# VectorE's masked copies as operations on two tensors, and a list schedule without a rule for a shared port

## The chip, the cores and the metric

The kernel runs on one core of a Trainium2 chip. The metric is the device time of one execution, in microseconds (us). The names of the engines are those of the profile: PE is TensorE (the matmuls, with PEld for its weight loads), DVE is VectorE, ACT is ScalarE, POOL is GpSimd, and SP is SyncE, which here issues the DMAs.

## The reference, cut to what matters

The input is 8 sequences of 512 tokens of width 256. Half a feed-forward block is added, then an attention block, then half of the same feed-forward block again. The "feed-forward block" holds an attention of its own, over the 16 heads of one token, whose keys and values are what the change touches.

```python
x = x + 0.5 * _L0_ffn_ref(_layernorm(x), ...)
x = x + _L0_attn_ref(_layernorm(x), ...)
x = x + 0.5 * _L0_ffn_ref(_layernorm(x), ...)

def _L0_ffn_ref(x, ...):                       # B=8 sequences, T=512, D=256, H=16, HD=16, E=8
    h = _rmsnorm(x, gamma1)
    q = (h @ Wq + bq).reshape(b, t, H, HD)
    kv = ((h @ Wdown + bdown) @ Wup + bup).reshape(b, t, H, 2 * HD)
    k, v = jnp.split(kv, 2, axis=-1)
    att = jax.nn.softmax(jnp.einsum('bthd,btgd->bthg', q, k) / sqrt(HD), axis=-1)
    out = jnp.einsum('bthg,btgd->bthd', att, v).reshape(b, t, D)
    x = x + (out @ Wo + bo)
    h2 = _rmsnorm(x, gamma2)
    gate = jax.nn.softmax(h2 @ Wg + bg, axis=-1)
    return x + jnp.einsum('btd,edf,bte->btf', h2, We, gate)
```

## The kernel before

**Jobs.** A job is one pass of the feed-forward block over one sequence. There are 16: jobs 0 to 7 before the attention block and 8 to 15 behind it. A job's 512 tokens are worked in two pairs of 128-token tiles, so that there are 32 pairs c = 0 to 31, with c = 2 * job + p. For each pair PE makes queries (step `q`, L448 with L453 for the bias) and keys and values (step `kv`, L448 with la and la_one). DVE turns them in blocks of 32x32: `q_turn` (L952) and `kv_turn` (L964 and L966, which write the tile kvcs).

**The masked copies.** The attention over heads is done with block-diagonal operands. The tile kvx holds, for each pair, eight blocks, and each block is a copy of half of kvcs, 128 partitions by 512 numbers, times a column of mask4, a 128x4 tile of zeros and ones. `EXPAND = "VPAAVPAV"` deals the eight copies out: three to DVE (step `expand_V`, L969), two to POOL (`expand_P`, L1390) and three to ACT (`expand_A`, L1165). When all eight are done PE multiplies queries and keys (`scores`, L613). DVE subtracts the maxima (`top`, L978 and L982), ACT exponentiates, PE turns (`turn_probs`, L708), ACT copies, PE multiplies by the values (`attend`, L624), and DVE divides (`mult`, L992 and L994). Output projection (`wo`), second norm and gating (`gate`, L448 with wg, `gateT` L755, `gate_sub` L1037 and L1039, `gate_soft` L1046 to L1055) follow.

**The experts.** The last product of a job has 16 `expert` steps, for four tiles i and four groups n, six matmuls of 512 columns each (L448, psum<-we,h). They use three PSUM banks in rotation: an expert step needs the bank that was filled three expert steps ahead of it to be read out. Steps with even n are read out by DVE (`add`, two instructions at L1067, which add into X), those with odd n by ACT (`y`, L1238). POOL then sums the y of a tile into X (`ysum`, L1421, L1423, L1426), and ACT's next `y` waits for that, since the tile y is reused.

**Other steps of POOL** that the prediction speaks of: `xs` (L1382, the first norm's scaling), `x1_base` (two at L1401, one at L1407), `norm` (L1344 to L1351, small operations and a power, L1349), `q_zero` (a memset, L1388), `we_lo` (L1372, eight operations that prepare the expert weights once). `half` is a DVE operation on two SBUF tensors (L1019). `h2_hi` (ACT, L1214) and `h2_lo` (DVE, L1027) copy the second norm's turned output out of PSUM, ahead of `gate` and the experts. In the attention block POOL's `normalise` (L1463) takes 3.9 us a time.

**What sets the order.** Each engine runs a fixed list of steps. The lists are made by a list scheduler on the host, `all_orders`, from a table of steps with an engine, a duration in ns and the steps that each waits for (`all_steps`). It goes forward in time and takes on each engine, of the steps that can start, the one with the longest chain behind it. The `expand_V` step stands in the table with 1900 ns. A rule named `port` lets no POOL step and none of the DVE steps `half`, `split_lo` and `expand_V` lie at the same time in the plan. The plan sets only the order: on the chip the semaphores decide when a step starts. The steps of the attention block follow one another by a list written out by formula; the feed-forward steps are placed around it.

## Time and profile before

| what | us |
|---|---|
| median of 3 runs | 1077.26 |
| lowest and highest | 1076.44, 1080.48 |
| the profiled execution, whole | 1075.92 |
| the profiled execution, span from its first instruction to its last | 1073.8 |

Busy time in the span: PE 1008.5 us (94%), DVE 864.4 (80%), POOL 746.5 (70%), ACT 648.4 (60%). A busy time is the union of an engine's instructions, so that an instruction that is held up while it runs counts as busy for all of it. TensorE's granted clock was 0.99 of full speed on average. A row of idle time names the instruction that waited and what released it last.

### The profile page before, as it was taken

To read this page: it belongs to the slowest core of one execution; us is meant where nothing else is said; L and a number is where in the kernel's file an instruction comes from. 1 tells how busy PE (TensorE), PEld (TensorE's weight loads), DVE (VectorE), ACT (ScalarE), POOL (GpSimd) and SP (SyncE) were. 2 spreads that over 40 slices of the span, in tenths; PEclk is the share of its full clock that TensorE was granted. 3 is DMA by queue.
4 is the path that set the end of the run, shared out by engine and by line. 5 is a ranking of instruction groups with operands and counts; after the bars stand their busy time and mean duration, and the time that the engine had idled before them with its cause. 6 is when DMAs were issued, how large, how long until landed. Compare 5 with 4: busy or idle time off the path is not lost.

```text
span 1073.8 us, 28494 instructions
## 1 busy us (share of the span) xinstructions
PE 1008.5 (94%) x11320; PEld 782.7 (73%) x11320; DVE 864.4 (80%) x1356; ACT 648.4 (60%) x1347; POOL 746.5 (70%) x743
## 2 busy tenths in 40 slices
PE   4789999999999989999999999877999999999997
PEld 3577888788788776666666666456878788788785
DVE  7888788787877459999999999988877787786852
ACT  4565564565654447777777777557654555655642
POOL 7667476675763449889889889995865574664544
PEclk9899999999999999999999999999999999999999
DMA  6110000000000000000000000000000000000000
GB/s 201 63 49 2 2 2 1 3 1 2 2 2 1 1 2 1 2 2 2 2 2 2 2 2 2 2 2 2 2 21 2 22 4 19 22 1 22 22 1 40
DMA packets 8410, 14.29 MB, mean 13 GB/s; under 512 B 2516, under 2 KB 6102, under 8 KB 8280
## 3 DMA queue, kind: packets, MB, share of 16 engines
q1 hardware_dynamic: 8280, 12.47, 3.5%
q8 instruction: 92, 1.51, 0.6%
q14 instruction: 38, 0.31, 0.1%
HBM read 8.28 MB, written 4.19 MB: 12 GB/s over the span
## 4 chain that ended last, share of the span: by engine, by line
PE 81%; DVE 8%; issue 5%; POOL 3%; ACT 1%; POOLq 0%; DVEq 0%; ACTq 0%
PE psum L448 54%; PE psum L816 5%; PE psum L826 5%; PE psum L842 4%; PE psum L613 3%; PE psum L624 3%; DVE late L1099 3%; DVE oT L1093 2%; PE psum L727 1%; PE psum L742 1%; PE psum L718 1%; PE psum L708 1%; PE psum L664 1%; DVE hT L1085 1%; POOL kvx L1463 1%
## 5 line engine op out<-in xcount | busy, mean ns | idle before, releaser
L448 PE MATMUL psum<-we,h 128*128 128x512 f32 x1536 | 396.6, 402 | 0.3 <-DVE X L1067 0.3
L448 PEld LDWEIGHTS psum<-we,h 128*128 128x128 f32 x1536 | 275.9, 188 | 59.4 <-issue 2.4
L1238 ACT ACTIVATE late<-psum,gate 128x256 f32<-128x256 f32 x256 | 107.2, 471 | 140.9 <-PE psum L448 96.2
L1421 POOL TENSOR_TENSOR late<-late 128x512 f32<-128x512 f32 x64 | 82.5, 1289 | 147.8 <-ACT late L1238 147.8
L1067 DVE SCALAR_TENSOR_TENSOR X<-psum,gate,X 128x256 f32<-128x256 f32 x256 | 122.8, 480 | 60.3 <-PE psum L448 48.3
L1288 ACT ACTIVATE kvx<-psum 128x1024 f32<-128x1024 f32 x128 | 131.3, 1026 | 64.3 <-PE psum L826 64.1
L1093 DVE TENSOR_REDUCE oT<-psum 128x128 fp32r<-128x1024 f32 x128 | 154.6, 1220 | 16.5 <-PE psum L816 16.1
L1099 DVE TENSOR_REDUCE late<-kvx 128x256 f32<-128x2048 f32 x64 | 145.7, 2277 | 0.0
L1463 POOL TENSOR_TENSOR kvx<-kvx,late 128x2048 f32<-128x2048 f32 x32 | 125.7, 3928 | 20.7 <-ACT late L1295 20.7
L1463 POOL TENSOR_TENSOR late<-kvx,late 128x2048 f32<-128x2048 f32 x32 | 125.2, 3914 | 15.8 <-ACT late L1295 15.8
L826 PE MATMUL psum<-oT,neg_id 128*128 128x512 f32 x256 | 89.1, 429 | 15.2 <-DVE oT L1093 14.6
L1165 ACT ACTIVATE kvx<-kvcs,mask 128x512 f32<-128x512 f32 x96 | 63.5, 741 | 6.8 <-PE psum L624 3.4
L826 PEld LDWEIGHTS psum<-oT,neg_id 128*128 128x128 f32 x256 | 40.5, 188 | 31.4 <-DVE oT L1093 22.3
L969 DVE TENSOR_SCALAR kvx<-kvcs,mask 128x512 f32<-128x512 f32 x96 | 63.0, 710 | 0.2
L1390 POOL TENSOR_SCALAR kvx<-kvcs,mask 128x512 f32<-128x512 f32 x64 | 47.1, 750 | 17.9 <-PE psum L624 10.7
L1180 ACT ACTIVATE at<-psum 64x256 f32<-64x256 f32 x128 | 48.5, 379 | 14.6 <-PE psum L708 13.3
L816 PEld LDWEIGHTS psum<-late 32*128 32x128 f32 x1024 | 37.1, 187 | 27.3 <-issue 27.3
L816 PEld LDWEIGHTS psum<-kvcs 32*128 32x128 f32 x1024 | 36.7, 185 | 26.6 <-issue 23.9
L1426 POOL TENSOR_TENSOR X<-X,late 128x256 f32<-128x256 f32 x64 | 47.2, 737 | 9.5 <-DVE X L1067 0.4
L448 PEld LDWEIGHTS psum<-wq,hT 128*128 128x128 f32 x384 | 50.7, 192 | 2.5
L816 PE MATMUL psum<-kvcs 32*128 32x128 f32 x1024 | 49.3, 295 | 3.1 <-ACT kvx L1288 2.2
L448 PE MATMUL psum<-wq,hT 128*128 128x256 f32 x384 | 51.2, 283 | 0.0
(153 smaller groups left out, 2010.3 us busy)
## 6 DMA issues: line engine op xcount, KB each, us to landing
X<-in_L_attn_hidden_states SPq DMA_DIRECT2D x8, 512.0 KB, 5.8
out<-X SPq DMA_DIRECT2D x8, 512.0 KB, 2.7
X<-in_L_ffn_We SPq DMA_DIRECT2D x2, 1024.0 KB, 10.6
kvx<-in_L_ffn_Wq SPq DMA_DIRECT2D x1, 256.0 KB, 3.0
kvx<-in_L_ffn_Wup SPq DMA_DIRECT2D x2, 128.0 KB, 3.1
kvx<-in_L_ffn_Wo SPq DMA_DIRECT2D x1, 256.0 KB, 4.2
X<-in_L_attn_Wk SPq DMA_DIRECT2D x1, 256.0 KB, 2.9
X<-in_L_attn_Wq SPq DMA_DIRECT2D x1, 256.0 KB, 3.2
```

Source lines behind the costliest of these rows:

```text
L448: ins = e.matmul(out_ap, l, r, start=(n == 0 and not opened), stop=(n == len(terms) - 1), skip_group_check=opened)
L816: ins = e.matmul(psum[:, pair(half) + bank, n * HQN:(n + 1) * HQN], qk[b % 2][rows, 1, hg, m * P:(m + 1) * P], qk[b % 2][rows, 0, hg, q0:q ...
L826: ins = e.matmul(psum[:, bank, :].rearrange("p (g n) -> p g n", n=HQN), neg_id[:, :], mr[g // 2 % 2][:, queries(g)].unsqueeze(1).to_broadc ...
L969: expand(e, k, "V", lambda o, src, m_: e.tensor_scalar(o, src, m_, None, ALU.mult))
L1067: e.scalar_tensor_tensor(out=xi, in0=psum[:, u % 3, w * D:(w + 1) * D], scalar=gate[k % 2][:, i, 2 * n + w:2 * n + w + 1], in1=xi, op0=ALU ...
L1093: e.tensor_reduce(mr[g // 2 % 2][:, queries(g)], heads(g), AX.X, ALU.max).then_inc(a_max, 1)
L1099: e.tensor_reduce(rec[u % 2][:, :], a_ex[u % EXR][:, :, :], AX.X, ALU.add).then_inc(a_total, 1)
L1165: expand(e, k, "A", lambda o, src, m_: e.activation(o, src, ACT.Copy, scale=m_))
L1238: e.activation(y[:, n // 2 * 2 + w, :], psum[:, u % 3, w * D:(w + 1) * D], ACT.Copy, scale=gate[k % 2][:, i, 2 * n + w:2 * n + w + 1]).the ...
L1288: e.activation(a_ex[u % EXR][:, queries(g), :], heads(g), ACT.Exp, scale=float(D) ** -0.5).then_inc(a_exp, 1)
L1421: own.step(e.tensor_tensor(y[:, 0:2, :], y[:, 0:2, :], y[:, 2:4, :], ALU.add))
L1463: e.tensor_tensor(prob[u % 2][:, :, :].rearrange("p g n -> p n g"), a_ex[u % EXR][:, :, :], rec[u % 2][:, :].unsqueeze(2).to_broadcast([P, ...
```

## The change

Two things change. DVE's three masked copies for each pair become `tensor_tensor` multiplications: the first operand is the half of kvcs as before, the second is the mask column, repeated 512 times by a stride of zero, in place of a per-partition scalar. Destination, count and size stay. And the rule `port` is taken out of the list scheduler, so that it may place DVE's `half`, `split_lo` and `expand_V` beside any POOL step. The duration table is as it was, 1900 ns for `expand_V` too. Six lines fewer stand above, so line numbers behind are lower by 6: L969 is L963, L1390 is L1384.

```diff
-    free = dict.fromkeys((*engines, "port"), 0)
+    free = dict.fromkeys(engines, 0)
...
-    def port(p):
-
-        return steps[p][0] == "POOL" or p[0] in ("half", "split_lo", "expand_V")
-
     def possible(p):
-        start = max(ready[steps[p][0]][p], free[steps[p][0]], free["port"] if port(p) else 0)
+        start = max(ready[steps[p][0]][p], free[steps[p][0]])
...
-        if port(p):
-            free["port"] = end[p]
...
                 elif name == "expand_V":
-                    expand(e, k, "V", lambda o, src, m_: e.tensor_scalar(o, src, m_, None, ALU.mult))
+                    expand(e, k, "V", lambda o, src, m_: e.tensor_tensor(o, src, m_.unsqueeze(2).to_broadcast([P, NR, HD]), ALU.mult))
```

The lists of DVE, PE, ACT and POOL all change. The first place is DVE in the middle jobs, from the turning of a job's first keys and values on. Before (L1067 is `add`, L969 the copies, L1027 `h2_lo`, L978 and L982 `top`):

```order
L964 STREAM_TRANSPOSE kvcs<-psum 128x16x32
L966 STREAM_TRANSPOSE kvcs<-psum 128x16x32
L952 STREAM_TRANSPOSE qc<-psum 128x16x32
L1067 SCALAR_TENSOR_TENSOR X<-psum,gate,X 128x256 x4
L964 STREAM_TRANSPOSE kvcs<-psum 128x16x32
L966 STREAM_TRANSPOSE kvcs<-psum 128x16x32
L952 STREAM_TRANSPOSE qc<-psum 128x16x32
L969 TENSOR_SCALAR kvx<-kvcs,mask 128x32x16 x3
L1027 SCALAR_TENSOR_TENSOR h<-psum,gam,h 128x256 x4
L969 TENSOR_SCALAR kvx<-kvcs,mask 128x32x16 x3
L978 TENSOR_REDUCE mx<-psum 128x32
L982 TENSOR_TENSOR late<-psum,mx 128x512
```

And DVE at the same place in the changed kernel (L1061 is `add`, L963 the copies, L1021 `h2_lo`, L972 and L976 `top`):

```order
L946 STREAM_TRANSPOSE qc<-psum 128x16x32
L1061 SCALAR_TENSOR_TENSOR X<-psum,gate,X 128x256 x2
L963 TENSOR_TENSOR kvx<-kvcs,mask 128x32x16 x3
L958 STREAM_TRANSPOSE kvcs<-psum 128x16x32
L960 STREAM_TRANSPOSE kvcs<-psum 128x16x32
L946 STREAM_TRANSPOSE qc<-psum 128x16x32
L1061 SCALAR_TENSOR_TENSOR X<-psum,gate,X 128x256 x2
L1021 SCALAR_TENSOR_TENSOR h<-psum,gam,h 128x256 x4
L972 TENSOR_REDUCE mx<-psum 128x32
L976 TENSOR_TENSOR late<-psum,mx 128x512
L963 TENSOR_TENSOR kvx<-kvcs,mask 128x32x16 x3
L1061 SCALAR_TENSOR_TENSOR X<-psum,gate,X 128x256 x2
```

The first pair's copies have moved up, ahead of the second `kv_turn`, and the second pair's have moved behind the first pair's `top`. Between the first `kv_turn` and the third `add` the set of steps is the same.

The second place is PE in the same stretch, from the turning of the second norm's output (L742, L736) on. L613 and L607 are `scores`, L708 and L702 `turn_probs`. Before:

```order
L742 MATMUL psum<-ident,late 128x128 x8
L448 MATMUL psum<-we,h 128x512 x12
L613 MATMUL psum<-kvx,qc 32x64 x32
L448 MATMUL psum<-we,h 128x512 x6
L448 MATMUL psum<-h,wg 8x512 x6
L613 MATMUL psum<-kvx,qc 32x64 x32
L755 MATMUL psum<-ident,ct 128x8 x4
L664 MATMUL psum<-ident,xs 128x128 x4
L448 MATMUL psum<-we,h 128x512 x6
```

PE there in the changed kernel:

```order
L736 MATMUL psum<-ident,late 128x128 x8
L442 MATMUL psum<-we,h 128x512 x6
L607 MATMUL psum<-kvx,qc 32x64 x32
L442 MATMUL psum<-we,h 128x512 x6
L442 MATMUL psum<-h,wg 8x512 x6
L442 MATMUL psum<-we,h 128x512 x6
L702 MATMUL psum<-ident,late 128x128 x4
L749 MATMUL psum<-ident,ct 128x8 x4
L658 MATMUL psum<-ident,xs 128x128 x4
L442 MATMUL psum<-we,h 128x512 x6
```

Ahead of the last expert step shown, the second `scores` is gone (it comes right behind it), and a `turn_probs` has come in.

The third place is POOL in the opening, around the copies of the third pair (L1390, L1384). Before:

```order
L1407 TENSOR_TENSOR late<-late,b_out 128x512
L1372 TENSOR_TENSOR we<-X,we 128x512
L1388 MEMSET qc 64x32x16
L1372 TENSOR_TENSOR we<-X,we 128x512 x3
L1390 TENSOR_SCALAR kvx<-kvcs,mask 128x32x16 x2
L1388 MEMSET qc 64x32x16
L1318 TENSOR_TENSOR wg<-raw_g,wg 128x16
L1372 TENSOR_TENSOR we<-X,we 128x512 x4
L1390 TENSOR_SCALAR kvx<-kvcs,mask 128x32x16 x2
```

POOL there in the changed kernel:

```order
L1366 TENSOR_TENSOR we<-X,we 128x512
L1444 TENSOR_SCALAR la_one<-la 64x512
L1366 TENSOR_TENSOR we<-X,we 128x512 x2
L1382 MEMSET qc 64x32x16
L1366 TENSOR_TENSOR we<-X,we 128x512 x3
L1384 TENSOR_SCALAR kvx<-kvcs,mask 128x32x16 x2
L1382 MEMSET qc 64x32x16
L1366 TENSOR_TENSOR we<-X,we 128x512 x2
L1384 TENSOR_SCALAR kvx<-kvcs,mask 128x32x16 x2
```

Six of the eight `we_lo` operations now stand ahead of the third pair's copies, where four did.

## Rows read from the trace of the kernel before

**Rows 1.** Busy times of the page, and a stretch (PE, PEld, DVE, ACT, POOL)

```profile
PE 1008.5 (94%) x11320; PEld 782.7 (73%) x11320; DVE 864.4 (80%) x1356; ACT 648.4 (60%) x1347; POOL 746.5 (70%) x743
...
176.00:219.00 43.00, 43.00 (x468) 35.23 (x468) 35.02 (x75) 24.52 (x60) 28.22 (x41) 1.00 0.01 2
```

**Rows 2.** Durations of two lines of DVE (ns: min/median/max)

```profile
L969 DVE TENSOR_SCALAR kvx<-kvcs,mask x96: 466/486/6749, 27.0 to 1011.3; 128x512 f32<-128x512 f32 x96
...
L886 DVE TENSOR_TENSOR wq<-kvx,wq x1: 693/693/693, 7.6 to 7.6; 128x512 fp32r<-128x512 f32 x1
```

**Rows 3.** Timeline of the opening: start, length, instruction, [idle before, releaser]

```profile
40.34 7.54 DVE L969 TENSOR_SCALAR kvx<-kvcs,mask 128x512 f32<-128x512 f32 x3
...
41.89 4.92 POOL L1372 TENSOR_TENSOR we<-X,we 128x512 fp32r<-128x512 f32 x4
...
48.10 1.93 PE L613 MATMUL psum<-kvx,qc 128*32 128x64 f32 x64 [5.97 <-issue]
```

**Rows 4.** Timeline: DVE operations on two SBUF tensors, and POOL beside them

```profile
63.55 1.29 POOL L1318 TENSOR_TENSOR aw<-X,aw 128x512 fp32r<-128x512 f32 x1 [1.73 <-ACT aw L1107]
...
64.51 0.87 DVE L1019 SCALAR_TENSOR_TENSOR X<-late,X 128x512 f32<-128x512 f32 x1
...
82.74 1.66 POOL L1349 TENSOR_TENSOR rs<-rs,half_neg 128x8 f32<-128x8 f32 x1
84.47 0.54 POOL L1351 TENSOR_TENSOR negm<-rs,negm 128x8 f32<-128x8 f32 x1
...
83.74 1.21 DVE L1019 SCALAR_TENSOR_TENSOR X<-late,X 128x1024 f32<-128x1024 f32 x1
```

**Rows 5.** Timeline at 314 us, where DVE's and POOL's copies coincide

```profile
314.32 2.41 DVE L969 TENSOR_SCALAR kvx<-kvcs,mask 128x512 f32<-128x512 f32 x3
314.70 1.75 POOL L1390 TENSOR_SCALAR kvx<-kvcs,mask 128x512 f32<-128x512 f32 x2
```

**Rows 6.** Timeline of DVE in a middle job

```profile
177.29 1.14 DVE L964 STREAM_TRANSPOSE kvcs<-psum 128x512 f32<-128x512 f32 x1
...
180.16 0.93 DVE L1067 SCALAR_TENSOR_TENSOR X<-psum,gate,X 128x256 f32<-128x256 f32 x2
181.69 1.00 DVE L1067 SCALAR_TENSOR_TENSOR X<-psum,gate,X 128x256 f32<-128x256 f32 x2 [0.60 <-PE psum L448]
...
185.59 1.98 DVE L969 TENSOR_SCALAR kvx<-kvcs,mask 128x512 f32<-128x512 f32 x3
...
189.11 1.36 DVE L969 TENSOR_SCALAR kvx<-kvcs,mask 128x512 f32<-128x512 f32 x3
...
191.78 0.99 DVE L1067 SCALAR_TENSOR_TENSOR X<-psum,gate,X 128x256 f32<-128x256 f32 x2
```

**Rows 7.** Timeline of PE in the same job, around the expert step that waits for that `add`

```profile
193.18 1.10 PE L613 MATMUL psum<-kvx,qc 128*32 128x64 f32 x64
194.21 0.41 PE L755 MATMUL psum<-ident,ct 8*128 8x8 f32 x4
...
194.97 1.63 PE L448 MATMUL psum<-we,h 128*128 128x512 f32 x6
196.44 0.60 PE L708 MATMUL psum<-ident,late 128*128 128x128 f32 x4
196.79 1.63 PE L448 MATMUL psum<-we,h 128*128 128x512 f32 x6
```

**Rows 8.** Timeline of POOL and ACT in the same job

```profile
181.50 1.43 POOL L1390 TENSOR_SCALAR kvx<-kvcs,mask 128x512 f32<-128x512 f32 x2
...
185.93 0.84 ACT L1238 ACTIVATE late<-psum,gate 128x256 f32<-128x256 f32 x2 [2.39 <-POOL X L1426]
```

**Rows 9.** Timeline of the return to the jobs

```profile
737.38 1.44 DVE L969 TENSOR_SCALAR kvx<-kvcs,mask 128x512 f32<-128x512 f32 x3
...
745.11 1.27 DVE L969 TENSOR_SCALAR kvx<-kvcs,mask 128x512 f32<-128x512 f32 x3
...
746.59 1.10 PE L613 MATMUL psum<-kvx,qc 128*32 128x64 f32 x64 [0.71 <-issue]
```

## The prediction

> **What bounds the kernel now.** I read the busy times and a table of stretches first. PE is busy 1008.5 us of 1073.8. In a middle job of 43 us it has no idle time at all, while DVE works 35.0 us of it and POOL 28.2 [rows 1]. So there a slower DVE costs nothing until one certain PE step has to wait for it, and then each microsecond of that wait is a microsecond of the whole. There are eight such equal periods, from 133 to 305 us and from 821 to 993 us, each with the copies of two pairs.
>
> The line of the copies comes next: 96 instructions, median 486 ns, longest 6749 ns [rows 2]. The long one is in the opening. DVE's three copies there take 7.54 us, POOL's chain of `we_lo` runs to 46.81 us, and PE stands for 5.97 us until the `scores` behind those copies can start at 48.10 [rows 3]. So the copies of today are held up by POOL. The question is whether the new ones are too, and what the new order makes of it.
>
> **The single operation.** The one two-tensor operation of 128x512 from SBUF in the trace takes 0.69 us, against 0.486 [rows 2]. Three copies took 1.27 us where nothing disturbed them [rows 9], which is 3 x 0.486 less 0.19 of overlap. Three new ones then take 3 x 0.69 - 0.19 = 1.88 us, 0.6 us more for each pair. All 32 pairs give 19.5 us more of DVE's work; only what lies on PE's path counts.
>
> **Is the new operation held up by POOL?** The trace has two DVE operations on two SBUF tensors beside POOL. At 64.51 us a `half` of 128x512 took 0.87, where the undisturbed two-tensor operation of that size took 0.69 [rows 2]: it ended at 65.38, and POOL's operation had ended at 63.55 + 1.29 = 64.84, 0.54 us ahead. In the other direction POOL's L1351, a 128x8 operation of 0.20 us, took 0.54 and ended at 85.01, when DVE's `half` had ended at 84.95 [rows 4]. So either makes the other wait, and DVE's 128x512 operation holds what they share for some 0.55 us. The shorter copy of today holds it less: at 314 us three copies and two of POOL's took turns for 2.41 us, POOL's two from start to end 1.75 [rows 5]. With 486 - 690/2 = some 0.28 us held for each DVE copy there, one of POOL's holds (1.75 - 2 x 0.28)/2 = 0.60 us.
>
> The Trainium skill (SBUF — State Buffer, "Who interferes with whom") says the same of these kinds: a VectorE instruction with two SBUF inputs contends with a GpSimd instruction that reads SBUF, and one that only writes it leaves it alone. It also says that the holder keeps the port for its whole instruction. The trace does not bear that out for every kind: `half` began at 83.74 inside POOL's L1349 (82.74 to 84.40) and took 1.21 us for 128x1024, less than twice 0.69 [rows 4]. By the page it would have waited the 0.66 us until POOL's end. None of the terms below rests on POOL's L1349.
>
> **The middle jobs, the largest term.** Follow the `add` that ends at 192.77 [rows 6]. The third expert step behind its own, which starts at 194.97 [rows 7], needs its bank. Between the first `kv_turn` at 177.29 and this `add` the new order has the same DVE steps. So their time is 192.77 - 177.29 = 15.48, less the copies' 1.98 and 1.36 and 0.60 of idle time: 11.54 us of other work [rows 6]. In PE's new order a `scores` is gone ahead of the expert step (194.21 - 193.18 = 1.03) and a `turn_probs` has come in (196.79 - 196.44 = 0.35) [rows 7]. PE gets there at 194.97 - 1.03 + 0.35 = 194.29. Both sets of copies together may take 194.29 - 177.29 - 11.54 = 5.46 us before PE stands.
>
> Undisturbed they take 3.76, and PE never waits. But they are not undisturbed. The first set moves up to 181.0, right behind the `add` of 180.16, and POOL's copies of the same pair start at 181.50 [rows 6, 8]. They take turns: 0.5 until POOL's running operation ends, 3 x 0.55 for DVE's and 2 x 0.60 for POOL's between them, 3.35 us. The second set meets `x1_base` or POOL's second copies, which stand there back to back in the new order: the same 3.35. The sum of 6.70 is 1.24 us over. On POOL's side each wait of 0.55 moves what is behind: `ysum` comes 1.65 us later, the `y` of ACT that waited for it (185.93, idle 2.39) as well [rows 8], and with it `h2_hi` and `h2_lo`, which stand behind that `y` and ahead of the second copies. DVE reaches `h2_lo` only 0.75 later by itself, so this adds up to 0.9. PE loses 1.24 to 2.1 us a period. I take 1.6, nearer to the end that DVE's own rows give. Eight periods: **+12.8 us**. The ends are 0 (nothing held, then 3.76 under 5.46) and 8 x 2.1 = 17.
>
> **The opening.** `we_lo` is POOL's chain of 1.23 us operations (4.92 / 4) [rows 3], and in the new order six of the eight stand ahead of the third pair's POOL copies. DVE's third set arrives inside that chain again. If they take turns, it lasts about 3 x (1.23 + 0.55) = 5.3 us in place of 7.54, but it begins later, since the first two pairs' sets are longer by 0.6 to 2 us each on a DVE that works nearly without a break there, and POOL's copies come two `we_lo` (2.5 us) later. The fourth set adds 0.6. I take **0**, with -5 (no stall) and +4 (a stall as long as today's, begun later) as ends.
>
> **The return from attention.** PE waits 0.71 us for the fourth set at 745.11; 1.27 becomes 1.88: +0.6. The third, at 737.38, took 1.44 [rows 9] beside POOL's copies; with one turn of POOL's it is 1.88 + 0.5, +0.9. **+1.5 us**, ends -1 (the new order has the first `scores` there in an idle stretch) and +3. The attention block has no copies, and its own steps keep their order: 0.
>
> **Sum.** 12.8 + 0 + 1.5 = +14.3 us on a span of 1073.8. Around the span lie 1075.9 - 1073.8 = 2.1 us, and the median is 1.3 above the profiled execution: 1077.3 + 14.3 = **1091.6 us**.
>
> **The rivals.** Taking turns, as summed, has 0.48: 1081 to 1100.
>
> No hold: a mask column that is read over and over might be fetched once, and then nothing is shared. For it speaks that no row has such an operand with both inputs in SBUF. The middle jobs then cost 0 and the long stall goes, which is up to the 5.97 us of PE, less 0.6 for each of the four sets of the opening, and the return costs 1.2. 1077.3 - 6 + 2.4 + 1.2 = 1074.9, same. 0.15. If the new order's earlier copies also bring PE's other waits of opening and return in, some 5 us more go: 1070, faster. 0.10.
>
> Half held: the two sets meet POOL's only once each in a period. Then they take 2 x 2.5 = 5.0 us, under 5.46, and only the chain over `ysum` is left, 0.6 us a period: 1077.3 + 5 + 1.5 = 1084. 0.15. It decides at 5.46 us for both sets.
>
> Starved: in the opening POOL had eight operations in a row while a copy waited (6749 ns). If that happens in the middle jobs, behind POOL's copies and `ysum`, each period costs 1.5 us more and the opening 4: 1091.6 + 12 + 4 = 1108. Against it: at 314 us they took turns [rows 5]. 0.12.
>
> **How the numbers follow.** A difference of 0.5% (5.4 us) is about what a measurement of this kernel can tell from none. Faster by more, under 1071.9: 0.11. Within: 0.17, from no hold and the lower edge of half held. Slower: 0.72. The range from 1073 to 1101 takes in no hold, half held and turns with their ends, and leaves the 0.10 and most of the 0.12 out.
>
> **What would show it.** DVE's copies last 3.0 to 3.5 us a set in the middle jobs and not 1.9; no single one is under 0.68. PE has 1 to 2 us of idle time in each middle period, released by `add` (L1061) or `h2_lo` (L1021), and the period is 44 to 45 us. If PE's middle periods stay at 43.0, the step on the hold or the 5.46 us is wrong. If PE waits, but for ACT's `y` or for `scores`, the place is wrong and the size a coincidence.

## The result

The changed kernel is slower, by more than the forecast said and beyond its range. It was timed twice, each time beside the kernel before on the same chip.

| | after, median (lowest to highest) | before, median | ratio, 95% interval |
|---|---|---|---|
| first | 1104.57 (1101.68 to 1106.85, 4 runs) | 1078.87 | 1.0232, 1.0184 to 1.0279 |
| again (`e5_after_again`) | 1103.15 (1102.00 to 1105.02, 4 runs) | 1081.97 | 1.0204, 1.0176 to 1.0232 |

That is 21 to 26 us where 14 were forecast. The profiled execution of the changed kernel took 1102.69 us with a span of 1100.6, against 1073.8 before.

The busy times of its page, and the stretch of one middle period, from the first expert step of job 4 to that of job 5 (columns as in [rows 1]):

```profile
PE 1018.2 (93%) x11320; PEld 786.9 (71%) x11320; DVE 893.0 (81%) x1356; ACT 649.3 (59%) x1347; POOL 777.9 (71%) x743
...
245.66:289.90 44.24, 43.37 (x467) 35.14 (x466) 37.56 (x75) 24.61 (x60) 30.42 (x41) 1.00 0.01 2
```

Against [rows 1], DVE is busy 28.6 us more and POOL 31.4 us more, though POOL has not one instruction more: it is held up. The period is 44.24 us, and PE has 0.87 us of visible idle time in it.

Where the time went, by the starts of the first expert step of the jobs (us). Before and after were each profiled twice, the second time as `e12_before_again` and `e5_after_again`, for which I had written:

> The kernel after once more, unchanged, on the chip of the runs beside it: 1102 to 1108 if the op and the order together cost what they did, where each alone cost 0.4 and 3.0 us; its first expert step at 68 to 73 us and its middle period at 44.2 us. A first expert step far from 71.5 would say that part of the +6.2 of the opening belongs to the one execution that was profiled.

> The kernel before once more, unchanged, for a second trace of it, since its runs lie between 1075 and 1085 us and the profiled one took 1075.9. If the opening and the attention are what differs from run to run: the middle period is 42.9 us again, and the first expert step lies at 65 to 69 us. If an execution differs anywhere else, the period shows it.

| stretch | before | after | more |
|---|---|---|---|
| to the first expert step of job 0 | 65.3, 64.9 | 71.5, 71.6 | +6.4 |
| jobs 0 to 2 | 82.0, 82.0 | 84.6, 84.7 | +2.7 |
| jobs 2 to 6 | 173.0, 173.2 | 178.2, 178.9 | +5.4 |
| jobs 6 to 7 | 33.6, 33.7 | 35.3, 35.3 | +1.7 |
| jobs 7 to 8, with the attention block | 399.1, 406.0 | 402.1, 400.3 | not told apart |
| jobs 8 to 10 | 82.6, 82.6 | 86.1, 86.1 | +3.5 |
| jobs 10 to 14 | 173.3, 173.6 | 178.3, 178.6 | +5.0 |
| jobs 14 to 15 | 34.7, 34.7 | 34.3, 34.3 | -0.4 |

The sum is 24 us. The +5.4 and +5.0 are not spread evenly: of four periods two lose 1.3 us each, one (jobs 2 to 3, or 12 to 13) loses 2.4 to 3.1, and the last loses 0.1 or nothing (44.4 us for jobs 5 to 6, against 44.3). Every stretch but one repeats to within 0.7 us. The exception is the one with the attention block, which differs by 7 us between two executions of the same kernel; in the slower of the two the granted clock was 0.67 from 710 to 730 us, where it had been 1.00. That fits the times of before, which lie anywhere from 1075 to 1086 us, though two traces do not show it for all of them. So I compare stretches, not totals, where a few microseconds matter.

The copies and the lines beside them, in after (ns: min/median/max):

```profile
L963 DVE TENSOR_TENSOR kvx<-kvcs,mask x96: 676/684/6929, 24.4 to 1032.3; 128x512 f32<-128x512 f32 x96
```
```profile
L1384 POOL TENSOR_SCALAR kvx<-kvcs,mask x64: 713/729/1745, 28.2 to 1035.8; 128x512 f32<-128x512 f32 x64
```
```profile
L1044 DVE TENSOR_SCALAR gs<-gs x18: 168/440/1807, 74.0 to 1073.5; 128x4 f32<-128x4 f32 x14, 128x2 f32<-128x2 f32 x4
```

A single copy costs what the forecast took, 0.68 to 0.69 us. POOL's copies are held to 1.75 us. And a third line stands out that the forecast never named: L1044, a DVE operation on 128x4 numbers in `gate_soft` (L1050 before), which takes up to 1.8 us.

### The profile page after: what moved, and what is told of

Same layout as the page of the kernel before. It is cut to its first block, busy times and chain, and to the rows that moved or that the text cites. A ratio compares the mean times of both kernels' runs of the same rounds, so it can differ in the third digit from the quotient of the medians.

```text
span 1100.6 us, 28494 instructions
## 1 busy us (share of the span) xinstructions
PE 1018.2 (93%) x11320; PEld 786.9 (71%) x11320; DVE 893.0 (81%) x1356; ACT 649.3 (59%) x1347; POOL 777.9 (71%) x743
## 4 chain that ended last, share of the span: by engine, by line
PE 55%; DVE 18%; POOL 13%; issue 9%; ACT 4%; POOLq 0%; DVEq 0%; ACTq 0%
PE psum L442 33%; PE psum L810 5%; PE psum L820 4%; PE psum L836 4%; DVE oT L1087 2%; DVE late L1093 2%; POOL xs L1376 2%; PE psum L618 2%; POOL rs L1343 2%; DVE kvx L963 2%; POOL kvx L1384 1%; PE psum L721 1%; DVE h L1021 1%; PE psum L607 1%; POOL late L1415 1%
## 5 line engine op out<-in xcount | busy, mean ns | idle before, releaser
L1415 POOL TENSOR_TENSOR late<-late 128x512 f32<-128x512 f32 x64 | 82.6, 1290 | 152.1 <-ACT late L1232 152.1
L1061 DVE SCALAR_TENSOR_TENSOR X<-psum,gate,X 128x256 f32<-128x256 f32 x256 | 121.8, 477 | 51.3 <-PE psum L442 40.0
L963 DVE TENSOR_TENSOR kvx<-kvcs,mask 128x512 f32<-128x512 f32 x96 | 79.8, 884 | 0.6
L1384 POOL TENSOR_SCALAR kvx<-kvcs,mask 128x512 f32<-128x512 f32 x64 | 64.5, 1022 | 15.8 <-PE psum L618 11.5
L820 PEld LDWEIGHTS psum<-oT,neg_id 128*128 128x128 f32 x256 | 40.5, 188 | 31.4 <-DVE oT L1087 22.3
L442 PEld LDWEIGHTS psum<-wq,hT 128*128 128x128 f32 x384 | 53.2, 201 | 2.6
L607 PE MATMUL psum<-kvx,qc 128*32 128x64 f32 x2048 | 37.8, 229 | 18.3 <-DVE kvx L963 7.6
L607 PEld LDWEIGHTS psum<-kvx,qc 128*32 128x32 f32 x2048 | 33.2, 116 | 30.0 <-issue 28.2
```

What stands on the lines that cost most here:

```text
L442: ins = e.matmul(out_ap, l, r, start=(n == 0 and not opened), stop=(n == len(terms) - 1), skip_group_check=opened)
L607: ins = e.matmul(psum[32 * j:32 * j + 32, keys[0], (2 * a4 + odd) * HALF:(2 * a4 + odd + 1) * HALF], queries_[:, r, :, :], keys[1][:, r, 0 ...
L820: ins = e.matmul(psum[:, bank, :].rearrange("p (g n) -> p g n", n=HQN), neg_id[:, :], mr[g // 2 % 2][:, queries(g)].unsqueeze(1).to_broadc ...
L963: expand(e, k, "V", lambda o, src, m_: e.tensor_tensor(o, src, m_.unsqueeze(2).to_broadcast([P, NR, HD]), ALU.mult))
L1061: e.scalar_tensor_tensor(out=xi, in0=psum[:, u % 3, w * D:(w + 1) * D], scalar=gate[k % 2][:, i, 2 * n + w:2 * n + w + 1], in1=xi, op0=ALU ...
L1415: own.step(e.tensor_tensor(y[:, 0:2, :], y[:, 0:2, :], y[:, 2:4, :], ALU.add))
```

## Experiment 1: each half of the change alone

The first question was which half does it. `e1_op_only` has the new operation and the rule, so that every engine keeps the order of before:

```diff
-                    expand(e, k, "V", lambda o, src, m_: e.tensor_scalar(o, src, m_, None, ALU.mult))
+                    expand(e, k, "V", lambda o, src, m_: e.tensor_tensor(o, src, m_.unsqueeze(2).to_broadcast([P, NR, HD]), ALU.mult))
```

> The kernel before with the operation changed alone: VectorE's copies are tensor_tensor with the mask repeated, and the port rule stays in the list schedule, so every engine has the order of before. If the moved order did the harm (my theory now: the surplus comes from POOL and VectorE steps that now stand side by side), this is within 4 us of before (1079 +- 4), a set of three copies lasts about 1.9 to 2.1 us alone and no VectorE copy takes over 2 us but the one of the opening. If the operation itself is dear (rival), it shows most of the +26: about 1095 to 1105.

`e2_rule_only` has the order of after and the old operation (the same line the other way round).

> The kernel after with the old operation: tensor_scalar copies in the order without the port rule. By the theory that the order does the harm, whatever the operation: 1095 to 1110, with the long first copy of the opening (6 to 8 us) and TENSOR_SCALAR L1044 (128x4) at 1 us on average as in after. By the rival that the new operation does it (it lets no POOL operation in between): within 5 us of before, 1074 to 1084.

Measured beside before at 1081.53 (19 runs): `e1_op_only` 1081.91 us (10 runs), ratio 1.0013 (0.9991 to 1.0036); `e2_rule_only` 1084.55 us (10 runs), ratio 1.0033 (1.0015 to 1.0051). So neither half costs the 21 us: 0.4 and 3.0 for each alone. My theory that the order does the harm whatever the operation fell here, and so did its rival. The stretches show it more closely (us more than the mean of the two traces of before):

| stretch | new operation alone | new order alone | both |
|---|---|---|---|
| to the first expert step | +4.1 | +3.8 | +6.4 |
| jobs 0 to 2 | 0 | +1.4 | +2.7 |
| jobs 2 to 6 and 10 to 14 | -2.2 | +0.4 | +10.5 |
| jobs 6 to 7 | +1.4 | +1.7 | +1.7 |
| jobs 8 to 10 | 0 | +2.4 | +3.5 |
| jobs 14 to 15 | +0.7 | -0.4 | -0.4 |

The new order alone costs 9 us here and 3 in the medians. The difference lies in the stretch with the attention block: it was 398.8 us in `e2_rule_only`, as short as the shorter one of before, and the ten times of that kernel lie within 2.4 us. The new operation alone costs 4.0 us here and 0.4 in the medians; its stretch with the attention block was 403.4 us, inside the 7 us of before, and cannot settle that. Outside the middle the two halves about add up: 15.0 us in sum against 13.8 for both, and to within 1.5 us in each stretch. In the middle they don't: alone they give -2.2 and +0.4, together +10.5. A middle period is 42.91 us in before, 42.65 with the operation alone, 42.63 with the order alone, and 44.24 with both:

```profile
236.47:279.12 42.65, 42.65 (x473) 35.15 (x467) 35.75 (x75) 24.46 (x60) 29.45 (x41) 1.00 0.01 2
```
```profile
238.70:281.33 42.63, 42.63 (x468) 35.12 (x466) 35.69 (x75) 24.48 (x60) 28.75 (x41) 1.00 0.01 2
```

(first `e1_op_only`, then `e2_rule_only`.) Both are bound by PE: 42.6 us of it, with no idle time. Each half's own delays on DVE and POOL are covered there. (Before has no visible idle time in its period either, and is 0.26 us longer: one expert step, at 241.74, starts 0.22 us later than in `e1_op_only`, where it is 244.87, by the same reckoning as in the next section. What it waits for there I have not traced.)

## How a middle period loses 1.6 us

`e2_rule_only` and after have the same instructions in the same order on every engine and differ in one operation. So their rows can be laid side by side, each counted from the start of its period (238.70 and 245.66). DVE and POOL around the two sets of copies of the period, and PE. First `e2_rule_only`:

```profile
227.41 1.35 POOL L1376 TENSOR_SCALAR xs<-X,rs,negm 128x256 f32<-128x256 f32 x2 [0.18 <-POOL negm L1345]
228.01 1.90 DVE L963 TENSOR_SCALAR kvx<-kvcs,mask 128x512 f32<-128x512 f32 x3
...
238.04 1.75 DVE L963 TENSOR_SCALAR kvx<-kvcs,mask 128x512 f32<-128x512 f32 x3
239.10 1.50 POOL L1395 TENSOR_SCALAR late<-X,rs,negm 128x256 f32<-128x256 f32 x2
239.72 0.99 DVE L1061 SCALAR_TENSOR_TENSOR X<-psum,gate,X 128x256 f32<-128x256 f32 x2
...
241.37 1.64 PE L442 MATMUL psum<-we,h 128*128 128x512 f32 x6
242.38 1.28 POOL L1415 TENSOR_TENSOR late<-late 128x512 f32<-128x512 f32 x1
242.94 1.10 PE L607 MATMUL psum<-kvx,qc 128*32 128x64 f32 x64
243.05 0.63 DVE L1044 TENSOR_SCALAR gs<-gs 128x4 f32<-128x4 f32 x1
...
247.82 0.60 PE L702 MATMUL psum<-ident,late 128*128 128x128 f32 x4
```

And after:

```profile
233.91 2.15 POOL L1376 TENSOR_SCALAR xs<-X,rs,negm 128x256 f32<-128x256 f32 x2 [0.18 <-POOL negm L1345]
234.51 2.09 DVE L963 TENSOR_TENSOR kvx<-kvcs,mask 128x512 f32<-128x512 f32 x3
...
245.44 2.32 DVE L963 TENSOR_TENSOR kvx<-kvcs,mask 128x512 f32<-128x512 f32 x3
245.50 1.74 POOL L1384 TENSOR_SCALAR kvx<-kvcs,mask 128x512 f32<-128x512 f32 x1
247.22 1.50 POOL L1395 TENSOR_SCALAR late<-X,rs,negm 128x256 f32<-128x256 f32 x2
247.68 0.99 DVE L1061 SCALAR_TENSOR_TENSOR X<-psum,gate,X 128x256 f32<-128x256 f32 x2
...
248.82 1.64 PE L442 MATMUL psum<-we,h 128*128 128x512 f32 x6 [0.25 <-DVE X L1061]
250.02 1.81 DVE L1044 TENSOR_SCALAR gs<-gs 128x4 f32<-128x4 f32 x1
250.51 1.29 POOL L1415 TENSOR_TENSOR late<-late 128x512 f32<-128x512 f32 x1
250.65 1.10 PE L607 MATMUL psum<-kvx,qc 128*32 128x64 f32 x64 [0.18 <-issue]
...
255.90 0.63 PE L702 MATMUL psum<-ident,late 128*128 128x128 f32 x4 [0.23 <-ACT late L1163]
```

The copies do not take turns one for one. DVE's second set is 2.32 us long, not 3.35: the first two copies run back to back (682 and 684 ns) while one POOL copy waits through both (1.74 us for 0.72). POOL gets in once, ahead of the third, which takes 1119 ns. PE's expert step that waits for L1061 starts at 248.82 - 245.66 = 3.16 us instead of 241.37 - 238.70 = 2.67: 0.49 lost. The next `scores` starts at 4.99 instead of 4.24: another 0.26.

L1415, the first addition of the job's last `ysum`, starts at 4.85 instead of 3.68. L1044 starts at 250.02, while POOL's L1401 still runs to 250.09. A memset of POOL and L1415 follow without a pause, and L1044 stands through them: it is done at 251.83, when L1415 has ended (251.80). The gate is ready late, and so are `add` and `y`; PE's `turn_probs` starts 0.38 later still. In before the same small operation took 0.17 to 0.25 us in all 18 places.

The first set of the period holds POOL too: `xs` L1376 x2 took 2.15 us beside it, against 1.35 in `e2_rule_only`. What follows from that is a chain over three engines, first in `e2_rule_only`, then in after:

```profile
277.43 1.10 PE L607 MATMUL psum<-kvx,qc 128*32 128x64 f32 x64
277.71 1.66 DVE L1021 SCALAR_TENSOR_TENSOR h<-psum,gam,h 128x256 fp32r<-128x256 f32 x4 [1.43 <-ACT h L1208]
...
279.95 1.54 PE L442 MATMUL psum<-h,wg 128*8 128x512 f32 x6
```
```profile
285.11 0.84 ACT L1232 ACTIVATE late<-psum,gate 128x256 f32<-128x256 f32 x2 [3.83 <-POOL X L1420]
...
285.64 1.10 PE L607 MATMUL psum<-kvx,qc 128*32 128x64 f32 x64
285.84 1.57 ACT L1208 ACTIVATE h<-psum,gam 128x256 fp32r<-128x256 f32 x4
...
286.71 1.66 DVE L1021 SCALAR_TENSOR_TENSOR h<-psum,gam,h 128x256 fp32r<-128x256 f32 x4 [2.11 <-ACT h L1208]
...
288.52 1.55 PE L442 MATMUL psum<-h,wg 128*8 128x512 f32 x6 [0.17 <-DVE h L1021]
```

POOL's `ysum` ends late, ACT's `y` waits for it, `h2_hi` stands behind that `y`, `h2_lo` waits for `h2_hi`, and `gate` on PE waits for `h2_lo`: 0.10 at the `scores` ahead of it, and 0.36 at `gate`. The five places give 0.49 + 0.26 + 0.38 + 0.10 + 0.36 = 1.59 us, the whole difference of 44.24 and 42.63. (In the last period of each four the difference is 0.2 us: the same delays arise, and PE makes them up again near the end of it.)

PE's idle time in brackets adds up to much less. A wait of a few tenths between matmuls lies largely inside PE's busy time, which grew by 0.74 us for the same matmuls. Two traces of one order are needed to find it.

## Experiment 2: the places one by one

**L1044.** `e3_no_halving` is after without this operation:

```diff
-                    own.step(e.tensor_scalar(gs[:, 0, own_t], gs[:, 2, own_t], 0.5, None, ALU.mult))
...
-                    e.tensor_tensor(g[:, own_t, :], gl[:, own_t, :], gs[:, 0, own_t].unsqueeze(2).to_broadcast([P, n, E]),
-                                    ALU.mult).then_inc(s_gate, 1)
+                    e.scalar_tensor_tensor(out=g[:, own_t, :], in0=gl[:, own_t, :], scalar=0.5,
+                                           in1=gs[:, 2, own_t].unsqueeze(2).to_broadcast([P, n, E]),
+                                           op0=ALU.mult, op1=ALU.mult).then_inc(s_gate, 1)
```

> The kernel after, with the small TENSOR_SCALAR L1044 of gate_soft (gs x 0.5, 128x4; 18 of them took 16 us in after where they took 3.4 us before) folded into the multiplication behind it, now a scalar_tensor_tensor with the scalar 0.5. Same result. If that operation's wait for a POOL operation beside it sets when the gate is ready, and so a middle period of 44.2 us (before 42.9), this gives back 0.8 to 1.2 us in each of 14 periods: 1090 to 1094. If the period is set by POOL's chain over ysum (L1420, y L1232, h2_hi, h2_lo), nothing is given back: 1102 to 1107. If the wait only moves to the next VectorE operation L1049: 1100 to 1106 and L1049 of 1.5 us.

1099.1 us against 1081.53 (ratio 1.0163, 1.0125 to 1.0201), middle period 43.87. The delay at `turn_probs` is gone (0.38), the other four are there as before. So the wait of L1044 has its price, but less than the 0.8 to 1.2 that I expected, and it is one place of five.

**POOL's place for `x1_base`.** `e8_ysum_first` moves one step on POOL alone:

```diff
+        line = orders["POOL"]
+        for s in range(2, 2 * B):
+            base, last = ("x1_base", s, 1), ("ysum", s - 2, NT - 1)
+            if s not in (B, B + 1) and line.index(base) < line.index(last):
+                line.remove(base)
+                line.insert(line.index(last) + 1, base)
```

> The kernel after with one step moved on POOL alone: x1_base(s, 1) (L1395 x2, L1401, 2.8 us) stands behind the last ysum of job s-2 instead of ahead of it, as in before; the other engines keep after's order. If the harm of the new order is that this step, with the copies that hold it up, stands ahead of the ysum that y L1232 and with it h2_hi and the next expert step wait for: a middle period of 42.7 to 43.3 us and a kernel of 1083 to 1092. If the place of that step is innocent: 44.0 to 44.3 and 1101 to 1107.

1098.43 us against 1081.97 (1.0157, 1.0131 to 1.0183), middle period 43.6. Gone are the delay at `turn_probs` (0.38) and the one at `scores` (0.26); 0.49, 0.10 and 0.36 stay. So the place of `x1_base` explains 0.6 us of the 1.6, not most of it as I expected. It explains the same 0.38 as L1044 does, since L1044 stood through a `ysum` that `x1_base` had made late.

**POOL's load.** `e7_pool_half` leaves out half of each of POOL's copies from set 4 on:

```diff
+                    if who == "P" and c >= 4:
+                        rows = slice(rows.start, rows.start + NR // 4)
```

> The kernel after with POOL's copies (L1384) of half the rows from set 4 on; the other half is left out, so the output of the later jobs is not the reference's. VectorE's copies are untouched. POOL gains 0.35 us a copy, 1.4 us a period. If the middle period is set by POOL's lateness (copies held through two or three of VectorE's, x1_base, ysum L1420, y L1232, h2_hi): it falls from 44.2 to 42.7 to 43.1, and the kernel to 1084 to 1090. If it is set by VectorE's own chain (the second set of 2.3 us ahead of add L1061): it stays at 43.9 to 44.3, and the kernel at 1100 to 1105.

1094.77 us against 1081.97 (1.0124, 1.0098 to 1.0151), middle period 43.4. The delays at `gate` and at the `scores` ahead of it are gone (0.46 together), and the first two are less than half (0.21 and 0.11 for 0.49 and 0.26). So the chain over `ysum` and `h2_lo` is real and costs 0.46, and it was the part that the forecast had described. The expected 42.7 to 43.1 was too low, since 0.37 at `turn_probs` stayed.

**DVE's second set ahead of `add`.** `e10_add_first` is e8 with one step more moved, on DVE:

```diff
+        line = orders["DVE"]
+        for s in range(2, 2 * B):
+            copies, add = ("expand_V", 2 * s + 1), ("add", s - 2, NT - 1, 2)
+            if s not in (B, B + 1) and line.index(copies) < line.index(add):
+                line.remove(add)
+                line.insert(line.index(copies), add)
```

> e8_ysum_first (middle period 43.6 us, 1098.4 us) with one more step moved, on VectorE: the last add of a job (L1061) stands ahead of the second set of copies instead of behind it. In after, and still in e8, the expert step that waits for this add starts 0.47 us later than in the kernel with the old operation, because the set ahead of the add takes 2.3 us where it took 1.75. If that is so: a middle period of 43.1 to 43.3 us and 1090 to 1096 for the kernel. If the set is not what the add waits for: 43.5 to 43.7 and 1097 to 1100.

1101.04 us against 1079.26 (1.0209, 1.0172 to 1.0246), middle period 43.5. The 0.49 at the expert step is gone, as expected. But the set comes 1 us later and meets `ysum` instead of `x1_base`. DVE and POOL in `e10_add_first`:

```profile
245.78 3.51 DVE L975 TENSOR_TENSOR kvx<-kvcs,mask 128x512 f32<-128x512 f32 x3
246.09 1.51 POOL L1427 TENSOR_TENSOR late<-late 128x512 f32<-128x512 f32 x1
...
247.68 1.07 POOL L1429 TENSOR_TENSOR late<-late 128x256 f32<-128x256 f32 x1
```

Now they do take turns for its last two copies, the set lasts 3.51 us, and `scores` is 0.33 late instead. The loss moved, and some other periods became longer (46.6 us for jobs 12 to 13, 45.5 in after). The place was right and the remedy worthless.

## Experiment 3: who gets in, and when

In after two of DVE's copies went through in a row while a POOL copy stood; beside `ysum` they took turns. `ysum` is where POOL waits for its own result between two operations. So `e9_gap` gives DVE such a wait:

```diff
+                    if who == "V" and ins is not None:
+                        dve_own.step(ins)
+                        e.wait_ge(dve_own.sem, dve_own.n)
```

> The kernel after with a wait of VectorE for its own copy ahead of the second and third copy of each set (L963), so that a copy is finished before the next is issued. If POOL's copies (L1384, 1.74 us in the second set of a middle job, 0.72 alone) are held because VectorE issues its copies back to back and takes the port again each time: with the waits they get in after one copy, at most 1.3 us each, and a set lasts 3 to 3.4 us, copy and copy in turns, so that the middle period is no shorter than 44.2. If the hold has nothing to do with the issue: L1384 keeps 1.7 us and the sets last 2.5 us (0.1 us more for each wait).

One run: 1105.04 us, middle period 44.0 to 44.1. In the middle jobs the longest POOL copy falls from 1.74 to 1.21 us, but more of them are held, 24 of 32 where 16 were:

```profile
L1388 POOL TENSOR_SCALAR kvx<-kvcs,mask x64: 712/1148/1303, 27.7 to 1035.9; 128x512 f32<-128x512 f32 x64
```

The sets last 2.70 and 2.77 us, less than the 3 us I expected for turns, but copies of 0.86 and 1.09 us show that POOL gets in between. So an engine that waits for its own result lets the other in; the sum of the two is about the same.

The reverse, that an engine which issues back to back keeps the other one out, is not shown, and often does not hold. In `e1_op_only` the same two POOL copies and three DVE copies meet, and none waits for a result:

```profile
234.69 1.97 POOL L1390 TENSOR_SCALAR kvx<-kvcs,mask 128x512 f32<-128x512 f32 x2
235.40 2.40 DVE L969 TENSOR_TENSOR kvx<-kvcs,mask 128x512 f32<-128x512 f32 x3
```

There the second POOL copy stood through one DVE copy only (1.28 us), and got in ahead of the second. In the other direction I took, in the trace of after, every place where a POOL operation ended beside a DVE copy that was being held, and the next POOL operation followed without a pause. There are 32. At 25 of them the copy got in, and six of the other seven belong to the one copy of 6.93 us in the opening. Where POOL paused for 0.08 to 0.23 us, the copy got in every time, in all the traces.

The long copy is in the opening. `e6_we_wait` is the kernel before with a wait of POOL between its `we_lo`:

```diff
                     e.wait_ge(s_hi, 7 + kk)
+                    if we_done:
+                        e.wait_ge(s_we, we_done)
+                    we_done += 1
```

> The kernel before with one thing added: ahead of each we_lo (POOL L1372, 128x512) POOL waits on the semaphore that the we_lo before it raises, so that it has finished before the next one is issued. In before, a VectorE copy of the opening took 6.7 us while eight POOL operations ran without a wait between them. If a waiting VectorE operation gets in only where POOL itself waits for something: that copy takes 1.3 to 2.6 us, the expert steps start 3 to 6 us earlier, and the kernel takes 1075 to 1079 where before takes 1081. If POOL's own gaps make no difference (rival): the copy still takes 5 to 8 us, and the kernel takes 1081 to 1083.

```profile
39.93 2.62 DVE L969 TENSOR_SCALAR kvx<-kvcs,mask 128x512 f32<-128x512 f32 x3
...
42.19 5.77 POOL L1376 TENSOR_TENSOR we<-X,we 128x512 fp32r<-128x512 f32 x4
42.75 1.10 PE L613 MATMUL psum<-kvx,qc 128*32 128x64 f32 x64 [1.03 <-DVE kvx L969]
```

The set of 7.54 us in [rows 3] takes 2.62, and PE's `scores` starts at 42.75 instead of 48.10. But the set is nearly over when the first of these `we_lo` starts (39.93 + 2.62 = 42.55, against 42.19). Its first two copies got in at 40.55 and 41.87 us, after a POOL copy and after a memset, and no new wait stands there. The set also began 0.4 us earlier than in before, against POOL's copies. So this run does not show that a held operation gets in only where the other engine waits; `e14_after_we_wait` below shows more. The worth of it is another thing. 1078.51 us against 1081.97 has a ratio of 0.9992 (0.9957 to 1.0027), so I ran it again:

> e6 once more (before with the wait between the we_lo): its first expert step came 2.0 us earlier than in before, but its ten times lay between 1072 and 1087. If that is all it gives: 2 us below before, ratio 0.997 to 0.999, and perhaps not to be told from no change. If the later opening has a price at the aw splits, which now stand beside PE's wait: 1.000.

1080.28 us against 1078.37, ratio 1.0020 (0.9997 to 1.0043), first expert step at 65.8. Of the 5.3 us that `scores` gained, 2.0 reached the first expert step in one execution and none in the other. Up to there PE is idle for 22.2 and 23.3 us, against 25.6 in before, but busy for 41.1 and 42.5 against 39.7 for the same 626 matmuls: 10.2 and 10.6 us of PE's work fell into stretches with the granted clock at half, where 7.0 did in before. It is no faster kernel. Nor is the same wait with the new operation in the order of before:

> The order of before, the new operation, and the wait between the we_lo of e6: meant as the fastest of those built so far. The new operation costs nothing in the middle there (42.7 us a period against 42.9), and the wait took the long copy of the opening from 6.7 to 1.4 us and the time to 1078.5 against 1082.0. If both hold together: 1076 to 1080 with before at 1082, ratio 0.994 to 0.998. If the gain of e6 was chance: 1081 to 1083.

1083.19 us against 1079.26, ratio 1.0042 (1.0014 to 1.0069), slightly above both ranges that I gave. No version that I ran beats the kernel before.

## Experiment 4: the opening

In after the first expert step comes 6.4 us late. `e4_rule_opening` keeps the rule for steps that the plan starts ahead of 60 us:

```diff
+        if port(p) and start < 60000:
+            start = max(start, free["port"])
```

> The kernel after with the port rule kept for steps that the list schedule starts before 60 us of its own time: the opening has the order of before on every engine up to about 75 us of the plan, the rest nearly the order of after. New copies throughout. If the opening's +6.2 us (first expert step 71.5 against 65.3) and the +2.6 of jobs 0 to 2 come from the moved order there: the first expert step is back at 65 to 66 and the kernel takes 1093 to 1099. If they come from the new operation: no change, 1101 to 1107.

1101.91 us against 1081.53 (1.0188, 1.0150 to 1.0225), first expert step at 68.8. So only 2.7 us came back, and the rest is the operation's: the first expert step is at 69.2 in `e1_op_only` and at 68.9 in `e2_rule_only`. Here the two halves come near to adding up (4.1 and 3.8 for 6.4). Not all of it is waiting. Up to the first expert step PE is idle for 25.6 us in before and for 29.6 in after; it is busy for 39.7 and 41.9. Some 1.1 us of that is work that moved: 64 matmuls more, as many as one `scores` has, stand ahead of this step in the new order. The rest goes with TensorE's granted clock: 8.7 us of PE's work fell into stretches with the clock at half in after, 7.0 in before. With the operation alone the clock is the larger part: `e1_op_only` has before's 626 matmuls up to there, and PE is idle for 26.1 us but busy for 43.0, of which 12.4 fell into such stretches. The trace of after shows two places of the waiting, POOL's steps ahead of its first copies and the third set:

```profile
24.29 2.55 POOL L1395 TENSOR_SCALAR late<-X,rs,negm 128x256 f32<-128x256 f32 x2
24.44 2.14 DVE L963 TENSOR_TENSOR kvx<-kvcs,mask 128x512 f32<-128x512 f32 x3
...
26.99 1.26 POOL L1401 TENSOR_TENSOR late<-late,b_out 128x512 f32<-128x512 f32 x1
...
30.30 1.94 PE L607 MATMUL psum<-kvx,qc 128*32 128x64 f32 x64 [4.73 <-POOL kvx L870]
...
42.63 3.75 POOL L1366 TENSOR_TENSOR we<-X,we 128x512 fp32r<-128x512 f32 x3
44.30 8.13 DVE L963 TENSOR_TENSOR kvx<-kvcs,mask 128x512 f32<-128x512 f32 x3
46.37 1.41 POOL L1384 TENSOR_SCALAR kvx<-kvcs,mask 128x512 f32<-128x512 f32 x2
...
48.20 2.48 POOL L1366 TENSOR_TENSOR we<-X,we 128x512 fp32r<-128x512 f32 x2
```

`e13_base_later` puts `x1_base(0, 1)` back behind POOL's first copies, and `e14_after_we_wait` is after with the wait of e6:

```diff
+        orders["POOL"].remove(("x1_base", 0, 1))
+        orders["POOL"].insert(orders["POOL"].index(("expand_P", 1)) + 1, ("x1_base", 0, 1))
```

> The kernel after with one step moved on POOL: x1_base(0, 1) (L1395 x2, L1401; 24.3 to 28.3 us in after, where one L1395 took 2.0 us beside VectorE's copies) stands behind POOL's first two sets of copies, as in before, instead of ahead of them. PE idles 4.7 us in after until POOL's first copies are done (scores(0) at 30.3 us). If this step is what holds them: scores(0) at 26 to 27.5 us, and the first expert step 1.5 to 3.5 us earlier than in after, 68 to 70. If another thing is late next (the copies of set 2, held through eight POOL operations): scores(0) as early, but the first expert step at 71 to 72.

> The kernel after with POOL's wait between the we_lo, as in e6. The first copy of set 2 took 6.9 us in after behind eight POOL operations. If the wait lets it in, as it did in e6: that copy at 1 to 2.7 us and the first expert step at 68 to 70, as much earlier as in before with the same wait (2 to 3 us). If it does not: 71 to 72.

First expert steps at 68.7 and 69.3 us, against 71.5, one run each: both as expected. In e13 PE's first `scores` starts at 28.11 instead of 30.30, earlier but not by as much as expected. In e14 the third set lasts 4.04 us instead of 8.13, with single copies of 1.77 and 1.75:

```profile
45.30 4.04 DVE L963 TENSOR_TENSOR kvx<-kvcs,mask 128x512 f32<-128x512 f32 x3
46.66 1.53 POOL L1370 TENSOR_TENSOR we<-X,we 128x512 fp32r<-128x512 f32 x1
48.17 2.37 POOL L1388 TENSOR_SCALAR kvx<-kvcs,mask 128x512 f32<-128x512 f32 x2
```

The first of these copies got in at the first pause of POOL, between the `we_lo` that ended at 46.52 and the one at 46.66; the first copy of the set of 8.13 us stood through seven POOL operations without one. The second got in at 48.19 with no pause at all (46.66 + 1.53, and POOL's next starts at 48.17). In e13 a set in the opening takes turns one for one, copies of 0.83, 1.78 and 1.75 us, beside POOL operations that follow one another without a pause:

```profile
31.43 4.21 DVE L965 TENSOR_TENSOR kvx<-kvcs,mask 128x512 f32<-128x512 f32 x3
31.87 1.54 POOL L1403 TENSOR_TENSOR late<-late,b_out 128x512 f32<-128x512 f32 x1
33.38 1.71 POOL L1368 TENSOR_TENSOR we<-X,we 128x512 fp32r<-128x512 f32 x1
```

So a pause lets the held operation in, and a row of operations without one is where the long stalls are, but what decides between turns and a stall in such a row stays open.

**All four.** `e15_all_four` has the changes of e13, e14, e8 and e3 in the kernel after.

> The kernel after (new operation, new order) with four small changes together: x1_base(0, 1) behind the first copies, the wait between the we_lo, x1_base(s, 1) behind the last ysum of job s-2 (e8), and L1044 folded into L1049 (e3). If these are the places where the loss arises: the first expert step at 66 to 69 us, a middle period of 43.2 to 43.5, and 1087 to 1093 us, with before at 1081. If the loss only moves to other places, as in e10: above 1095.

1090.17 us against 1078.37 (ratio 1.0103, 1.0071 to 1.0135), the first expert step at 65.8, the middle period 43.6. So half of the loss is back: nearly all of the opening's, and 0.6 us of each middle period. In the middle periods folding L1044 in gives nothing on top of e8. At jobs 8 to 10 it gives 2.0 us: 84.1 us here and in e3, 86.1 in e8 and in after. What is left is 0.49, 0.10 and 0.36 of each middle period, and 2.5, 1.7 and 1.5 us in jobs 0 to 2, 6 to 7 and 8 to 10. The new order alone brings most of these (table of experiment 1). Which of its moves does, I haven't tried; it stays open.

## Why the prediction was wrong

- **The direction and the size of the largest term were right.** Jobs 2 to 6 and 10 to 14 are, but for a shift of some 14 us, the eight periods of the forecast. They lost 10.5 us, forecast 12.8: 1.3 us each on average and not 1.6. The period is 44.2 us, inside the 44 to 45 that I gave.
- **But it came by another way than the term says, and the near size is in good part luck.** The step "take turns" failed. It read the 2.41 us of [rows 5] as one-for-one; the sets are 2.09 and 2.32 us, not 3.35 each, together 4.4 and under the 5.46 us at which DVE alone would stop PE. The 5.46 failed too: it counts no wait of DVE ahead of `h2_lo`. With the 2.1 us of after the two sets make 6.5 us, and PE waits for `add`; with the 1.4 us of `e2_rule_only` they make 5.1 us, and it does not. What came true is the second part of that step, the chain over `ysum`, `y` and `h2_lo`, and at 0.46 us it is only a piece. I gave "released by `add` (L1061) or `h2_lo` (L1021)", and both are there, and they take 0.85 of the 1.59 us. The rest is at `scores` (0.36) and `turn_probs` (0.38), of which I had written that the place would then be wrong and the size a coincidence. In the order of before the same copies are covered (`e1_op_only`): the new order had used up the lead of DVE and POOL over PE.
- **The opening was the failed term: 0 forecast, +6.4 measured.** Two things stood in it. The copies' stall did not shrink to 5.3 us, since DVE did not take turns with this chain of POOL operations, which has no wait in it; it stayed, as in [rows 3], and the new set took 8.13 us. I had named this as the rival "starved" and priced the opening in it at +4. And I did not look at POOL ahead of the first pair's copies, where `x1_base` had moved in. Nor did the term count the granted clock: 1.7 us more of PE's work ran at half clock in after, and 5.4 us more with the new operation alone.
- **Jobs 0 to 2, 6 to 7 and 8 to 10 were not costed**, but for 1.5 at the return: +7.8 measured. I read the moved order at three places and took the rest for neutral. The order alone costs 5.5 us there, and of the 3.5 us at jobs 8 to 10 the wait of L1044, which no term had, makes up 2.0 (`e3_no_halving`).
- **The rival "no hold"** is excluded by POOL's copies of 1.75 us and DVE's of 6.9, and "half held" by its size, though its picture of the middle, two sets well under 5.46 us and a loss by the chain, is the nearest.
- **The single operation, 0.69 us, and three for 1.88** were right (0.684, and 1.88 where nothing is beside them). The mistake was never in the operation's own time. One figure beside it is miscalculated: 486 - 690/2 is 141 ns, not 0.28 us. The 0.28 itself is what the rows show, since a held copy of the old kind ends 0.28 us after the POOL operation ahead of it, and one of the new kind 0.52 to 0.55.
- The Trainium skill's sentence (SBUF — State Buffer, "Who interferes with whom") that the holder keeps the port for its whole instruction, and that the other is blocked, is borne out in after by L1044, which ended with the POOL operation beside it. Who comes next when both have more to do is what decided here. The runs show a part of it: a pause of the holder lets the other in. What decides without a pause, they leave open.

## What to carry to other kernels

Two changes that are each free in a loop cost 3% of it together here (10.5 us of 347), because both are paid from the same spare time: ask of a harmless change how much of the cover it uses up, and time the parts apart and together. Where two engines exclude each other, look for long rows of operations without a wait: each stall of 5 us or more stood beside one, though most such meetings passed in turns. An operation that needs a result of its own engine lets the other in. When a scheduler's rule goes, every place where the plan moved is a term of the sum, not only the largest.

## What the runs showed of the hardware

- A DVE operation waited 6.2 us (6929 ns for one of 684) for seven POOL operations that were issued one after another, and a memset among them did not let it in; with a wait of POOL for its own result between them it took 1765 ns. Issue in a row is not enough for such a stall: in the same trace DVE's copies got in at 25 of 32 places without a pause.
- In the other direction a POOL operation waited through two DVE operations in a row, 1.74 us for one of 0.72, and in the order of before through one, 1.28 us.
- The second operand with a stride of zero, one column read 512 times, costs what two full tensors do: 0.68 us, against 0.69 for the one operation of that size on two full tensors, and it is held up by POOL.
- A DVE operation on 128x4 numbers (L1044, one SBUF tensor and a constant), 0.17 us alone, took 1.81 us when it stood through the end of one POOL operation, a memset of 0.52 and an operation of 1.29. Its size is no protection.
- In the attention block and at the return two executions of the same kernel differ by 7 us, with TensorE's granted clock at 0.67 or at 1.00 over 20 us behind idle stretches of PE.
